# Five uneven rounds of row tiles in the middle blocks, row sums of x at the head, and six norm groups instead of five

## What is computed

```
u = par_u[0]*par_u[1] * (diag_u[:,None] * x[:2048]  @ W_u) + x[:2048]
i = par_i[0]*par_i[1] * (diag_i[:,None] * x[2048:]  @ W_i) + x[2048:]
e = concatenate([u, i])
h = adj @ (adj.T @ e)
L0 = (h - mean(h)) * rsqrt(var(h) + 1e-5) * gamma + beta + x
x1 = layernorm(x + L0)
out = layernorm(x1 + L1(x1, adj))
```

## Time and profile before

| | us |
|---|---|
| median of 3 runs | 415.06 (414.4 to 415.21) |
| the profiled execution | 414.27 |
| its span, first to last instruction | 412.5 |
| TensorE matmul busy | 383.8 (93%) |
| VectorE busy | 324.7 (79%) |
| ScalarE busy | 266.6 (65%) |
| GpSimd busy | 68.6 (17%) |
| granted TensorE clock, mean | 0.985 of 2.4 GHz |
| read from HBM | 107.60 MB |

### The profile page before, as it was taken

How to read it: one execution, slowest core, us unless ns; L and a number is a source line. 1 busy time by engine, 2 the same in 40 slices (tenths; PEclk the granted TensorE clock), 3 DMA queues, 4 the chain that set the end, 5 groups by cost and what they waited for, 6 DMA issues and landing times.

```text
span 412.5 us, 13885 instructions
## 1 busy us (share of the span) xinstructions
PE 383.8 (93%) x6018; PEld 223.2 (54%) x6018; DVE 324.7 (79%) x404; ACT 266.6 (65%) x497; POOL 68.6 (17%) x122
## 2 busy tenths in 40 slices
PE   8987999999999999999999999999999999999940
PEld 7543555565464455546445554644555464668740
DVE  3699769799695979769786966988696697694783
ACT  3696938799888488578848857884785688100220
POOL 2001100303003000300200030011003001169663
PEclk9999999999999999999999999999999999999995
DMA  8999999954992998399389929957992995400002
GB/s 293 386 387 381 386 386 387 382 217 144 388 386 109 322 387 314 114 388 385 138 289 379 354 83 373 387 184 260 385 370 55 392 386 202 130 4 3 29 27 82
DMA packets 56706, 109.87 MB, mean 266 GB/s; under 512 B 3776, under 2 KB 3904, under 8 KB 56640
## 3 DMA queue, kind: packets, MB, share of 16 engines
q1 hardware_dynamic: 56352, 108.84, 72.6%
q10 hardware_dynamic: 288, 0.09, 0.1%
HBM read 107.60 MB, written 1.31 MB: 264 GB/s over the span
## 4 chain that ended last, share of the span: by engine, by line
PE 51%; DMA 23%; SPq 18%; DVE 2%; issue 2%; POOL 1%; ACT 0%; DVEq 0%; ACTq 0%
PE pair L1382 39%; DMA pooled<-in_adj 22%; SPq L977 17%; PE pair L1363 10%; PE pair L1395 2%; DMA pooled<-in_x 2%; POOL pooled L1052 1%; DVE pooled L1204 1%; SPq L968 1%; DVE pooled L1182 1%; SPq L963 1%; POOL pooled L1047 0%; DVE pooled L1272 0%; DVE pooled L1264 0%; DVE pooled L1293 0%
## 5 line engine op out<-in xcount | busy, mean ns | idle before, releaser
L1086 ACT ACTIVATE scratch<-pooled 128x1024 bf16<-128x1024 f32 x200 | 210.5, 1053 | 63.8 <-DMA pooled<-in_adj 61.9
L1182 DVE STREAM_TRANSPOSE pooled<-pooled 128x1024 f32<-128x1024 f32 x200 | 228.8, 1208 | 11.3 <-ACT scratch L1086 8.9
L1363 PE MATMUL pair<-pooled,rows_in 128*64 128x256 f32 x1600 | 186.0, 383 | 10.7 <-DMA pooled<-in_adj 10.3
L1382 PE MATMUL pair<-pooled,col_sum 32*64 32x320 f32 (+3 forms) x4224 | 177.4, 485 | 0.9 <-DVE pooled L1204 0.5
L1363 PEld LDWEIGHTS pair<-pooled,rows_in 128*64 128x64 f32 x1600 | 109.6, 137 | 88.4 <-DMA pooled<-in_adj 31.1
L1382 PEld LDWEIGHTS pair<-pooled,col_sum 32*64 32x64 f32 x4224 | 94.0, 132 | 78.7 <-issue 57.0
L1204 DVE TENSOR_TENSOR pooled<-pooled,pair 128x320 f32<-128x320 f32 (+3 forms) x120 | 58.1, 545 | 44.6 <-PE pair L1382 44.6
L1022 POOL COPY col_sum<-col_half 32x256 f32<-32x256 f32 x80 | 31.6, 394 | 317.6 <-DVE col_half L1191 314.6
L1095 ACT COPY col_sum<-col_half 32x256 f32<-32x256 f32 x80 | 32.2, 403 | 11.1 <-DVE col_half L1191 10.3
L1086 ACT ACTIVATION_READ_ACCUMULATOR scratch<-pooled 128x1 f32 x200 | 37.4, 187 | 0.0
L1113 ACT ACTIVATE pooled<-pair 128x512 f32<-128x512 f32 x5 | 3.0, 598 | 39.3 <-PE pair L1395 39.3
(11 more groups left out here) (47 smaller groups left out, 62.2 us busy)
## 6 DMA issues: line engine op xcount, KB each, us to landing
pooled<-in_adj SPq DMA_DIRECT2D x200, 512.0 KB, 10.1
pooled<-in_x SPq DMA_DIRECT2D x5, 256.0 KB, 3.7
out<-pooled SPq DMA_DIRECT2D x5, 256.0 KB, 2.0
pooled<-in_x SPq DMA_DIRECT2D x1, 768.0 KB, 6.9
pooled<-in_x SPq DMA_DIRECT2D x1, 512.0 KB, 3.7
pooled<-in_w_ui ACTq DMA_DIRECT2D x1, 64.0 KB, 2.9
beta_sb<-in_beta SPq DMA_DIRECT2D x1, 32.0 KB, 9.0
pooled<-in_scales ACTq DMA_DIRECT2D x1, 22.0 KB, 3.2
```

The lines of the kernel that those rows point to most:

```text
L1086: nc.scalar.activation(scratch[v % 2][:, :], slots[slot_of(v)], ACT.Square, accum_out=square_sum[:, v:v + 1]).then_inc(unit_scanned, 1)
L1182: nc.vector.transpose(tiles, tiles).then_inc(unit_turned, 1)
L1363: mm = pe.matmul(block_bank[c % 2][half(h), 0:w // 2], rows_in[:, t, :], slots[slot_of(v)][:, at:at + w // 2], start=(t == 0), stop=(t == ...
L1382: mm = pe.matmul(round_banks(g)[a][half(b % 2), 0:w].rearrange("p (t r) -> p t r", r=32), col_sum[c % 2][quadrant(a), b, :], to[quadrant(a ...
```

## The change

- Rounds. Blocks 1 to 7 get five rounds of 4, 6, 8, 8 and 14 tiles instead of three of 10, 14 and 16. Block 8 gets 6, 10, 10, 14 instead of four of 10. Block 9 gets 8, 8, 8, 8, 4, 4 instead of five of 8. Block 0 keeps its three. VectorE's hand-written order follows; in block 0 `turn_half` stands before the last 4 units and not before the last 2.
- Row sums of x. The one `tensor_reduce` over the second copy of x (L1251, in block 8) goes; five of 8 tiles each over the first copy stand in VectorE's head queue (two before `make_e(0)`, three after `make_e(2)`), and SP waits for them before it overwrites that copy. GpSimd waits for the second copy itself, for the second round of block 8, writes epsilon columns, and then centres all five groups of x before its first power.
- Norm groups. They follow the rounds of block 9: six groups, the last two of 4 tiles. The squares are scaled by ScalarE, and a 65th column that holds epsilon is summed along, so that the two `tensor_scalar` operations (L1266, L1285) of each group go. Waits for `c_summed` and `y_summed` on ScalarE become waits two groups back.
- Outputs. `make_out` of groups 0 to 3 is done by ScalarE, one copy with a scale for each tile, into four buffers instead of two; groups 4 and 5 stay on VectorE.

```diff
-    PARTS = [((0, 10), (10, 14), (24, 16))] * (NB - 2)
-    PARTS += [tuple((t, 10) for t in range(0, T, 10)), tuple((t, 8) for t in range(0, T, 8))]
+    PARTS = [((0, 10), (10, 14), (24, 16))]
+    PARTS += [((0, 4), (4, 6), (10, 8), (18, 8), (26, 14))] * (NB - 3)
+    PARTS += [((0, 6), (6, 10), (16, 10), (26, 14)), ((0, 8), (8, 8), (16, 8), (24, 8), (32, 4), (36, 4))]
...
+        c_sq = [ln_buffer(D + 1) for _ in range(2)]
+        y_sq = [ln_buffer(D + 1) for _ in range(2)]
+        ln_t = [ln_buffer(D) for _ in range(2)]
+        ln_o = [ln_buffer(D) for _ in range(4)]
...
                     sp.wait_ge(e_made, LGROUPS)
+                    sp.wait_ge(x_summed, LGROUPS)
...
-            for k in range(LGROUPS - 1):
+            pool.wait_ge(round_done, ROUNDS_AT[NB - 2] + 2)
+            for k in range(2):
+                nc.gpsimd.memset(c_sq[k][:, :, D:D + 1], LN_EPS).then_inc(eps_put, 1)
+                nc.gpsimd.memset(y_sq[k][:, :, D:D + 1], LN_EPS * LN_EPS).then_inc(eps_put, 1)
+            for k in range(LGROUPS):
                 center_x(k)
+            pool.wait_ge(x_steps, 1 + 3 * LGROUPS)
             root_c(0)
-            pool.wait_ge(rstd_made, 1)
-            center_x(LGROUPS - 1)
-            pool.wait_ge(x_steps, 1 + 3 * LGROUPS)
             root_c(1)
...
+            def make_out(k):
+                act.wait_ge(scale_made, k + 1)
+                for i in range(norm_size(k)):
+                    t = norm_tiles(k).start + i
+                    made = nc.scalar.activation(ln_o[k % 4][:, i, :], x_all[:, t, :], ACT.Copy, scale=scale[:, t:t + 1])
+                made.then_inc(out_made_act, 1)
...
+            def sum_x(k):
+                dve.wait_ge(x_loaded[k], 16)
+                nc.vector.tensor_reduce(x_sum[:, group_tiles(k)], x_first[:, group_tiles(k), :], X,
+                                        ALU.add).then_inc(x_summed, 1)
...
-            for v in range(7, UPB[0] - 2):
+            for v in range(7, UPB[0] - 4):
                 turn_unit(v)
             turn_half(0)
-            for v in range(UPB[0] - 2, UPB[0]):
+            for v in range(UPB[0] - 4, UPB[0]):
                 turn_unit(v)
...
-                for v in range(first + 13, first + 15):
-                    turn_unit(v)
-                add_round(ROUNDS_AT[c])
-                if c < NB - 2:
-                    for v in range(first + 15, UNIT_FIRST[c + 2]):
-                        turn_unit(v)
+                turn_unit(first + 13)
...
+                else:
+                    add_round(ROUNDS_AT[c])
+                    turn_unit(first + 14)
                     add_round(ROUNDS_AT[c] + 1)
...
+                    turn_unit(first + 15)
+                    turn_unit(first + 16)
                     add_round(ROUNDS_AT[c] + 2)
...
+                    turn_unit(first + 17)
+                    turn_unit(first + 18)
                     add_round(ROUNDS_AT[c] + 3)
+                    turn_unit(first + 19)
+                    add_round(ROUNDS_AT[c] + 4)
...
             multiply_round(LAST + 4)
             close_tiles(3)
+            multiply_round(LAST + 5)
             close_tiles(4)
+            close_tiles(5)
```

More of the change, by code:

```diff
@@ L113, in adjacency_layers_kernel, with ln_buffer @@
         x_all = pooled[:, x_at:x_at + T * D].rearrange("p (t d) -> p t d", d=D)
[L114 to L126, removed]
+        var, rstd, y_var, y_eps, x1_rstd, scale = (
+            pooled[:, x_at + T * D + T * i:x_at + T * D + T * i + T] for i in range(6))
+        ln_at = x_at + T * D + 6 * T
+        ln_end = [ln_at]
+        def ln_buffer(width):
+            ln_end[0] += GT * width
+            return pooled[:, ln_end[0] - GT * width:ln_end[0]].rearrange("p (t d) -> p t d", d=width)
+        c_sq = [ln_buffer(D + 1) for _ in range(2)]
+        y_sq = [ln_buffer(D + 1) for _ in range(2)]
+        ln_t = [ln_buffer(D) for _ in range(2)]
+        ln_o = [ln_buffer(D) for _ in range(4)]
+        assert ln_at <= x_at + CH * PARTS[NB - 2][0][1] and ln_end[0] <= x_at + CH * sum(PARTS[NB - 2][1])
         rows_in = sb("rows_in", [P, T, D])
@@ L249, in adjacency_layers_kernel @@
         x1_steps = sem("x1_steps")
+        out_made_act = sem("out_made_act")
         out_made = sem("out_made")
-        out_stored = [sem(f"out_stored{k}") for k in range(2)]
+        out_stored = [sem(f"out_stored{k}") for k in range(4)]
         max_found = sem("max_found")
@@ L984, in _ @@
                 sp.dma_start(x_all[:, a:b, :], tile_rows(x, a, b - a)).then_inc(x_again, 16)
[L986 to L990, removed]
+            for k, (first, nt) in enumerate(PARTS[NB - 1]):
+                if k < BY_ACT:
+                    sp.wait_ge(out_made_act, k + 1)
+                else:
+                    sp.wait_ge(out_made, k - BY_ACT + 1)
+                sp.dma_start(tile_rows(out, first, nt), ln_o[k % 4][:, 0:nt, :]).then_inc(out_stored[k % 4], 16)
+            for k in range(4):
+                sp.wait_ge(out_stored[k], 16 * len(range(k, NORMS, 4)))
             with sp.If(edges_may_survive(sp) > 0):
@@ L1209, in _ @@
             make_e(2)
+            for k in range(2, LGROUPS):
+                sum_x(k)
             for v in range(3):
@@ L1321, in _ @@
             nc.vector.tensor_scalar(flag[0:1, :], all_max[0:1, :], LIMIT, None, ALU.is_ge).then_inc(flag_made, 1)
-            make_out(4)
+            for k in range(BY_ACT, NORMS):
+                make_out(k)
             with dve.If(edges_may_survive(dve) > 0):
@@ L1388, in close_tiles @@
             def close_tiles(k):
[L1390 to L1395 removed]
+                first, nt = PARTS[NB - 1][k]
+                pe.wait_ge(round_added, LAST + k + 1)
+                if 2 <= k < 5:
+                    pe.wait_ge(t_made, k - 1 if k < 4 else 3)
+                for i in range(nt):
+                    mm = pe.matmul(nat_of(k)[:, i, :], h_sum[:, P * (first + i):P * (first + i) + P], center[:, :],
                                    start=True, stop=True)
```

128 lines of the change are left out of this document (68 added, 60 removed).

## The result

The changed kernel took 449.91 us (median of 4 runs, 448.99 to 452.36) against 414.73 us for the kernel before (4 runs, 412.41 to 415.21): a ratio of 1.085 between the medians, and of 1.087 as estimated from all these runs, 95% interval 1.081 to 1.093. The forecast was 403 us, with a range up to 411. The profiled execution took 450.32 us, its span 448.5.

The account below looks back on a forecast made before the run. TensorE was busy 93%, but late loads set the unit stretches' end in blocks 3 to 9. Span 412.5 - 9.7 (periods) - 2.3 (tail) = 400.5 us; plus 1.8 and 0.8 gave 403 us, range 398.5 to 411.

Parts of the forecast that it names:

- The waits for loads: Blocks 1 to 8: late loads cost 1.76 us a period, 12.3 us in all; an earlier first release would remove them.
- period of 35.2 us: Blocks 1 to 7: TensorE would set the period at 35.2 us, for 36.64 before; with block 2's wait, 9.7 us gained.
- 1.2 us of slack: Blocks 1 to 7: the period by loads would be 34.0 us, 1.2 us below TensorE's 35.2.
- Small rounds run at their columns' rate: Blocks 1 to 7: a 4-tile round takes 1.9 us, with bursts of 120 ns.
- rival (a): Small rounds bound by instructions at 26.9 ns each: 4- and 6-tile rounds take 3.45 us, 424 us in all; chance 0.13.
- The length of the round stretch: Blocks 1 to 7: the rounds of a block would take 17.7 us, say 17.75, for 17.46 before.
- VectorE's slack: Blocks 1 to 7: five adds cost 7.1 us for 6.4; 0.4 us of waiting left; `turn_half` delays block 2 by 0.4 us once.
- The tail: Block 8's rounds to the end: a gain of 2.3 us, from 0 to 4.
- The head: Start of the kernel: five row sums of 0.69 us each would add 0, up to 0.5 us if not covered.

Follow-up runs that it names:

- e5: Changed kernel with three rounds of 8, 16 and 16 tiles in blocks 1 to 7: 419.1 us, ratio 1.008.
- e1: Kernel before with only the rounds of blocks 1 to 7 changed to 4, 6, 8, 8 and 14 tiles: 451.37 us, ratio 1.091.
- e2: Changed kernel with blocks 1 to 7 back at rounds of 10, 14 and 16 tiles: 411.5 us, ratio 0.996.
- e3: Changed kernel with each load of adj bringing 64 of its 512 columns from block 3 on: 415.99 us.
- e4: Changed kernel with four rounds of 6, 10, 10 and 14 tiles in blocks 1 to 7: 443.2 us, ratio 1.073.
- e9: Changed kernel with five rounds of 8 tiles in blocks 1 to 7: 455.21 us.
- e8: Changed kernel with the five rounds of blocks 1 to 7 put between the units of the next block: 443.41 us, ratio 1.068.

## Why the prediction was wrong, point by point

**The waits for loads** were read rightly: 12.3 us were seen in them, and all 12.3 went. But that they would have gone at a period of 35.2 us, with the 1.2 us of slack that the prediction gives the loads, isn't shown: the period here is 42.3 us, so the loads had 7 us more than forecast. In e5, where TensorE did not slow down, an early release did make the queue pause.

**Small rounds run at their columns' rate**: right where instructions are at hand. In a 4-tile round of the tail (windows as in the earlier trace rows) 71 instructions start in 1.00 us, 14.1 ns each, 113 ns a burst against the 120 taken:

```profile
430.52:431.00 0.48, 0.47 (x32) 1.00 0.27 90
430.52:432.00 1.48, 1.47 (x103) 1.00 0.49 180
```

So the floor of rival (a), 26.9 ns an instruction for every small round, isn't there. The Trainium skill's floor of about 25 ns from start to start ("TensorE: Matmul & The Clock Gate", section "Wait — 56ns, not 53.3ns?") doesn't hold for matmuls that alternate between places of the array: this run has 14.1 ns.

**The length of the round stretch is the step that failed**: "Rounds of a block then take 17.46 + 32 more bursts x 2.5 ns (0.08) + 0.17 ... = 17.7 us". Measured were 21.5 to 28.1 us, 24.9 in the mean, 7.1 us a period more, 50 in all, and 35.5 of the 50 are gaps that end with an instruction packet. The sum priced each instruction by its columns and its weight load and left out that it has to be brought. Two more rounds are 512 more instructions a block, and the supply, three blocks of 256 in 17.5 us before, had to be five. Rival (a) said "twice the rate of anything seen is asked of the queue"; that sentence was the right one, but I priced it as a floor for each small instruction, which would have spared rounds of 8 tiles, and gave it 0.13. Its price, 424 us, was 26 below the result for the same reason. A hint stood in the rows: the last 8-tile round before was interrupted (its last part starts at 391.28 in the chain that the earlier trace rows is cut from, behind 0.41 us of "issue", after 89 instructions), far from any semaphore, and 1.20 us after the end of an instruction packet.

**VectorE's slack** held where it could be tested: from the fifth add to the next `turn_half`, which the gaps don't lengthen, it waited 0.53 us for the last unit where 0.4 were forecast (0.54 in the row above), and the wait for `turn_half` in the first period was 0.37 us for 0.4. The adds between the rounds had more time than in the plan, so they prove nothing.

**The tail**: a gain of 4.2 us in this profile for 2.3 (0 to 4). Sizes were off, in the right direction: a power of 4 columns took 1.0 us, as taken, but standing alone an 8-tile round took 3.64 us for 3.95 and a 4-tile one 2.03 for 2.3. The end of the chain:

```profile
389.05 24.32 PE pair L1429 x768
...
426.59 2.03 PE pair L1429 x124
...
442.00 0.42 DVE pooled L1338
```

The kernel with everything but the rounds shows that this gain isn't firm: there the gaps fell into the last rounds, and 1.7 us were left.

**The head** was forecast at 0 to 0.5 us and is 0.6 us longer. That is within what varies between executions: block 1's rounds start at 92.34 in the kernel before and at 93.29 in e1, which has the same head, and at 92.60 to 93.61 in the profiles with the new head (the kernel after, e2, e3, e4, e5 and e9).

## What to carry to other kernels

Cutting matmul work into more, smaller pieces costs instructions, and an engine's instructions have a supply of their own: count them per microsecond in each stretch, as bytes are counted, and not over the whole kernel only (e8). Gaps put down to nothing, in the middle of a group and 256 instructions apart, are its sign, and packets of the instruction queue that end just ahead of each resumption prove it. If a load comes late because its slot is released late, move the use that releases it between other work before making that use smaller.

## What the runs showed of the hardware

- TensorE's instructions (matmuls and weight loads counted) came in blocks of 256. Where they were short, one block came every 4.2 to 6.9 us with the DMA at 240 to 365 GB/s (kernel after), and in 3.8 us at the least with loads an eighth as large (e3). Each block is one packet of 16.4 KB of the instruction queue, 0.9 to 1.6 us long. All 84 gaps for instructions (0.2 us or more) of the kernel after, e1, e3 and e9 end 1.25 to 1.61 us after the end of such a packet. Beside full loads the packet starts later; why is not shown.
- In block 8's rounds and the two behind them, where almost nothing was loaded but x, 768 matmul instructions passed in 24.32 us without a gap, a block of 256 in 4.1 us.
- After 2.2 to 2.8 us without a matmul the granted clock fell to the lower level (1.2 GHz) for some microseconds in several periods (kernel after, e1, e9). In e4 it did so behind five of seven waits of 2.4 us and cost 1.4 to 1.8 us each time.
- An instruction that only waits, put between matmuls that use different places of the array, held them back: with two ahead of each of 192 matmuls (384 matmul instructions) the stretch went from 17.46 to 45.9 us, 148 ns more a matmul. A matmul instruction itself took as long as before (a median of 0.51 us in either), so fewer of them were under way at a time.
